# At most four gathers under way in a decoder's routed experts

## What is computed

```python
def _L0_ffn_ref(x, Wg, W1, W2, W3):
    scores = xt @ Wg.T
    topk_scores, topk_idx = jax.lax.top_k(scores, TOP_K)
    gate = jax.nn.silu(jnp.einsum('td,ehd->teh', xt, W1))
    up = jnp.einsum('td,ehd->teh', xt, W2)
    y = jnp.einsum('teh,edh->ted', gate * up, W3)
    onehot = jax.nn.one_hot(topk_idx, E, dtype=x.dtype)
    w = jnp.einsum('tke,tk->te', onehot, topk_scores)
    out = jnp.einsum('te,ted->td', w, y)
    return out.reshape(B, S, D)
...
    x = x + _L0_ffn_ref(_layernorm(x, axis=-1), L0_ffn_Wg, L0_ffn_W1, L0_ffn_W2, L0_ffn_W3)
```

## Time and profile before

| | us |
|---|---|
| median of 3 runs | 1053.18 |
| lowest and highest run | 1051.42, 1053.36 |
| the profiled execution | 1051.36 |
| its span, first to last instruction | 1049.6 |

### The profile page before, as it was taken

The page is one execution under the profiler, slowest core; times in us unless marked ns, Lnnn a source line. Parts: engine busy times, 40 slices in busy tenths (PEclk is TensorE's granted clock), DMA queues, the critical chain, the costliest instruction groups (busy, mean ns, idle before and its releaser), DMA issues. The chain is left out here.

```text
span 1049.6 us, 16519 instructions
## 1 busy us (share of the span) xinstructions
PE 901.8 (86%) x5273; PEld 728.0 (69%) x5274; DVE 640.3 (61%) x1142; ACT 466.1 (44%) x824; POOL 640.3 (61%) x528
## 2 busy tenths in 40 slices
PE   6967667999979999889998899985299999998664
PEld 4534344666856587665787668875299999998654
DVE  4199688887887967976888231573144444443226
ACT  2565755667765568745675123221032333332111
POOL 2178897899977999868998110047465346545250
PEclk8989886999979999979999999988599999999777
DMA  9560022000180000520004000527331333112132
GB/s 319 181 222 0 1 81 81 9 9 1 43 280 1 17 1 1 216 108 17 1 1 161 2 15 2 188 87 228 75 103 53 125 125 125 40 40 75 55 95 96
DMA packets 49405, 86.00 MB, mean 82 GB/s; under 512 B 6420, under 2 KB 39080, under 8 KB 47304
## 3 DMA queue, kind: packets, MB, share of 16 engines
q1 hardware_dynamic: 43352, 66.03, 18.5%
q0 software_dynamic: 6000, 19.29, 6.1%
HBM read 66.16 MB, written 14.55 MB: 77 GB/s over the span
## 5 line engine op out<-in xcount | busy, mean ns | idle before, releaser
L459 POOL TENSOR_TENSOR u<-dtx,b_all 128x512 f32<-128x512 f32 x256 | 332.5, 1310 | 69.0 <-DVE h L722 65.4
L722 DVE TENSOR_TENSOR_SCAN h<-da,u 128x512 f32<-128x512 f32 x256 | 308.8, 1216 | 46.4 <-ACT da L543 21.4
L543 ACT ACTIVATE da<-dt_,a_neg 128x512 f32<-128x512 f32 x256 | 175.0, 690 | 111.1 <-DVE h L722 110.3
L863 PEld LDWEIGHTS ysum<-ident,h 128*128 128x128 f32 x800 | 100.7, 151 | 54.1 <-issue 26.7
L863 PE MATMUL ysum<-ident,h 128*128 128x128 f32 x800 | 117.3, 291 | 17.8 <-DVE h L722 7.7
L1355 ACT ACTIVATE act_<-ps_g 128x352 f32<-128x352 f32 x78 | 36.0, 464 | 150.7 <-PE ps_u L1630 88.9
L1041 PE MATMUL pv<-pT,ctx_n 128*128 128x128 f32 (+1 forms) x832 | 101.3, 275 | 1.1 <-ACT pT L617 1.1
L1041 PEld LDWEIGHTS pv<-pT,ctx_n 128*128 128x128 f32 (+1 forms) x832 | 97.7, 192 | 5.0 <-issue 1.5
L1012 PE MATMUL pa<-ctx_t,xnT_a 128*128 128x401 f32 (+1 forms) x256 | 95.6, 510 | 1.7 <-ACT xnT_a L601 1.4
L1653 PE MATMUL ps_y<-w_hi,hidT_hi 128*128 x234 | 67.1, 287 | 20.6 <-issue 17.8
L1501 DVE TENSOR_TENSOR hid<-act_,ps_u 128x352 f32<-128x352 f32 x78 | 40.3, 517 | 70.5 <-ACT act_ L1355 41.5
(11 more groups left out here) (224 smaller groups left out, 1856.1 us busy)
## 6 DMA issues: line engine op xcount, KB each, us to landing
b_all<-b_dram SPq DMA_DIRECT2D x16, 1024.0 KB, 4.7
ctx_t<-in_ctxT SPq DMA_DIRECT2D x4, 1601.0 KB
ctx_n<-in_ctx SPq DMA_DIRECT2D x4, 1536.0 KB
ffn_sorted<-yg SPq DMA_DIRECT2D x1, 4992.0 KB, 22.6
ffn_sorted<-y_sb SPq DMA_DIRECT2D x39, 128.0 KB
tok_in<-tok SPq DMA_DIRECT2D x35, 128.0 KB, 2.0
mask<-in_mask SPq DMA_DIRECT2D x16, 200.1 KB, 2.4
w_raw<-in_w1T SPq DMA_DIRECT2D x4, 704.0 KB
```

What stands on the lines that cost most here:

```text
L459: nc.gpsimd.tensor_tensor(u[:, i % 2, :], dtx[:, j % 2, :], b_all[:, n, :], ALU.mult).then_inc(u_ok, 1)
L543: nc.scalar.activation(da[i % DS][:], dt_[:, j % 2, :], ACT.Exp, scale=a_neg[:, j, n:n + 1]).then_inc(da_ok, 1)
L722: nc.vector.tensor_tensor_scan(h[:, i % HS, :], da[i % DS][:], u[:, i % 2, :], 0.0, ALU.mult, ALU.add).then_inc(scan_ok, 1)
L863: last = nc.tensor.matmul(ysum[:, t * P:(t + 1) * P], h[:, i % HS, t * P:(t + 1) * P], ident[:], is_transpose=True, start=first and t == 0 ...
```

## The change

```diff
--- before.py
+++ after.py
@@ -1184,6 +1184,7 @@
         PAIRS = 4
         tok_ld = [sem(f"tok_ld{n}") for n in range(PAIRS)]
         AHEAD = 4
+        UNDER_WAY = 4
...
-        low_ld, up_ld, comb = sem("low_ld"), [sem(f"up_ld{g}") for g in range(G // 2)], sem("comb")
+        low_ld, up_ld, comb = [sem(f"low_ld{n}") for n in range(2)], [sem(f"up_ld{g}") for g in range(G // 2)], sem("comb")
...
@@ -1308,8 +1309,8 @@
                 pool.wait_ge(id_ok, 1)
                 for i in range(NT):
 
-                    if i % 2 == 0 and i >= 2 * PAIRS:
-                        pool.wait_ge(tok_ld[i // 2 % PAIRS], gathered(i - 2 * PAIRS))
+                    if i % 2 == 0 and i >= UNDER_WAY:
+                        pool.wait_ge(tok_ld[(i - UNDER_WAY) // 2 % PAIRS], gathered(i - UNDER_WAY))
                     pool.indirect_dma_start(tok[:, i, :], None, xn3_dram,
...
-                def fetch(y, k, done):
+                def fetch(y, k, done, done_before):
                     for g in range(G):
+                        if g % 2 == 0 and g >= UNDER_WAY:
+                            done_before(g - UNDER_WAY)
                         pool.indirect_dma_start(y[:, g, :], None, ffn_sorted,
...
-                fetch(y_one, 0, lambda g: low_ld)
+                fetch(y_one, 0, lambda g: low_ld[g // 2 % 2], lambda g: pool.wait_ge(low_ld[g // 2 % 2], 32 * (g // 4 + 1)))
                 stored(1)
-                fetch(y_two, 1, lambda g: up_ld[g // 2])
+                fetch(y_two, 1, lambda g: up_ld[g // 2], lambda g: pool.wait_ge(up_ld[g // 2], 32))
...
-                    dve.wait_ge(low_ld, 16 * G)
+                    for n in range(2):
+                        dve.wait_ge(low_ld[n], 16 * G // 2)
```

## The result

The changed kernel took 1045.51 us (median of 20 executions; 1037.0 to 1051.89 apart from two, of 1522.42 and 2237.25 us, that the comparison leaves out), the kernel before 1052.7 us beside it (20 executions, 1047.34 to 1054.35). The ratio is 0.9934, 95% interval 0.9916 to 0.9952: 0.7% faster. My forecast of 1054.2 us was wrong, and so was its range, which began at 1048.5.

A forecast was written before the change was run, and what follows sets the result against it. TensorE bounds the expert phase, with three holes under unbroken gathers (56.2 us). Later hole end +4.6, pauses giving back 1.6 and 2.0: +1.0 us, forecast 1054.2 us; own range 1052 to 1055.5, range to hold 1048.5 to 1059.

The forecast's parts named there:

- Three holes bound the kernel: Expert phase: TensorE paces it, except 26.62, 13.96 and 15.58 us when it nearly stands under token, lower and upper gathers.
- itself has the time: GpSimd after the token gathers: a later last gather costs it nothing, since its next work waits until 765.33 for TensorE.
- Lower and upper waits: Twelve new waits in the lower and upper gathers: all already met, cost 0, holes of 13.96 and 15.58 us stay.
- Token waits of 4.6 us: Token gathers beside two weight loads: gathers 6, 12 and 14 wait 2.3, 0.8 and 1.5 us; last starts at 754.4.
- The later end of the hole: Token gathers: Silu again follows the last gather by 3.8 us, so the first hole ends 4.6 us later, +4.6 us.
- What the pauses give back: Token gathers: waits let the other engines catch up, 1.6 us in the first pause and 2.0 us in the later ones.
- 3.0 us of release: Time ScalarE needs to be let go after the last lower gather; taken as what a pause must last to clear everything.
- run-in: Stretch from the first gather after a pause to TensorE's last regular matmul: 12.3, 9.4 and 9.0 us; begins anew at 724.3.
- a standstill clears it: Token gathers: GpSimd's standstill of 5.4 us, from the gather at 711.62 to 717.02, cleared the other engines' delay.
- Rival 1: Token gathers: pauses shorter than the release clear next to nothing, the hole ends later; +2.1 to +5 us, chance 0.34.
- Rival 2: Token gathers: the new run-in lets one more tile through before the stand; 1049.5 to 1051 us, chance 0.14.
- Rival 3: All gathers: missing spacing holds the engines, new waits loosen it everywhere, all holes shrink; halved, about 1025 us, chance 0.12.

The follow-up runs named there:

- half gathers: Kernel before with 64-row lower gathers and tiny operations behind the eighth upper gather: 1053.52 us on a chip with holes, 995.31 and 993.93 us without.
- two under way: Changed kernel with at most two gathers under way, not four: 1051.66 us, ratio 1.0011 with holes; 1050.48 us, 1.0665 without.
- spread kernel: Changed kernel, two token gathers under way, placed between weight splits; lower and upper in groups of four: 993.85 us, 0.9461 with holes; 989.92 us, 1.0042 without.
- plain loads: Kernel before with lower gathers as plain loads without indices and tiny operations between upper gathers: 991.55 and 999.52 us, both on chips without holes.

## Why the prediction was wrong, by its own steps

- **Three holes bound the kernel, and nothing else is late.** Right for the chips with holes. What I said of GpSimd, that it "itself has the time", rests on them: it waits 14.59 us for TensorE only because TensorE stood for 26. In the kernel before on a chip without holes it goes on at once, 0.01 us after the last token gather, and there the waits count in full.
- **Lower and upper waits cost nothing, and their holes stay.** Right: gaps of 0.30 us throughout, holes of 14.6 and 12.8 + 4.3 us, and 1.0001 for these waits alone.
- **Token waits of 4.6 us.** Mis-sized: 10.3, or 9.1 without the usual gaps. Gather 6 waited 4.53 for 2.3, gather 10 3.25 for none, gather 12 1.25 for 0.8, gather 14 1.27 for 1.5. I took the 192nd packet of the queue for the last one of the first four gathers. A pair is complete only when all of its packets are, and those of later gathers can be through before; that is argued from the late releases, no run singled it out. The Trainium skill, "DMA: Bandwidth & Descriptors", section "Queues, rings and completion order", has each of the 16 DMA engines work through a ring of its own and take turns with other queues packet by packet; that fits, since the slowest of the rings then sets a pair's landing, and no view here shows it ring by ring. The last gather came at 757.08, not at 754.4; 7.3 us late and not 9.1, since the first one was 0.6 us early and VectorE's split cost GpSimd 1.2 us less than before.
- **The later end of the hole.** The rule was right, 4.0 us after the last gather for 3.8; with the larger waits it is 7.5 us and not 4.6.
- **What the pauses give back.** The step that failed. I let a pause clear a share of the delay, by its length over the 3.0 us of release, and found 3.6 us, with 6.1 as the end. Two more tiles got through: the fifth tile is 5.2 us early (0.6 of it from the earlier first gather) in spite of an end 7.5 us later, so some 12 us came back, near two tiles (13.5). With pauses of 4.53, 3.25, 1.25 and 1.27 us in a row ScalarE never fell behind: Silu at 728.45 waits for TensorE alone. The run-in then begins anew as I had it, 726.78 to TensorE's hole at 735.34, 8.6 us for 9.0; but I counted one such run-in, where four pauses kept the engines going throughout. How much one pause of 1.3 us clears by itself no run singled out. Nor was "a standstill clears it", read from one gather, safe: in the half gathers' last trace 5.4 us of it cleared nothing. Rival 1, with the same rule of shares at zero, fell with it. Rival 2, a whole tile, had the mechanism and was still too small; it had a chance of 0.14.
- **Rival 3**, spacing helps everywhere: not by the met waits. Yet real spacing does clear all three holes, as the kernel with two under way shows; my argument against it was right only for this change.
- **The new wait.** I named nothing that would be late once the hole is shorter. It was the copy of a tile beside GpSimd's reload of weights, 8.14 us in the chain, and it took back 3.9 of the 5.2 us in the profiled execution. Why other executions keep more, down to 1037 us, stays open: they weren't traced. The last down projection at the lower clock is 1.7 us of it here. A part may come from ahead of the experts, where the first token gather starts anywhere from 686.8 to 696.5 us in the traces of the kernels that are the same up to there, on both kinds of chip.

## What to carry to other kernels

Before a stall of tens of microseconds is charged to the kernel's own order, time the same kernel on another chip: this change is worth -0.7% of the time on one and +1.1% on another. A pause in a stream of gathers can be cheap or dear; what decides is what the issuing engine has to do next and who waits for that. Put the pauses where that engine has slack, here behind the splits of weights that are needed first, and the gain of 5.4% on the one kind of chip costs 0.4 to 0.6% on the other. The spread kernel is right only for these lists of tokens: were the experts ahead of a split to need more tiles than have been gathered, the split would wait for TensorE and TensorE for a gather behind the split, for ever.

## What the hardware showed that I had not expected

- Of the last six sets, two on two chips gave 1052 and 1055.5 us for the kernel before, and four on three chips 986 to 987 us; the chip that came twice was without holes both times, and no chip with holes is on record twice. So that it is the chip, and not what else ran on it or how it was set up at the time, is the nearest reading and not shown. The first two comparisons, both with holes, had 1052.7 and 1051.0. The two traces of the kernel before differ by 68.5 us of span. By the copies of results, the stretch of the token gathers lost 30.4 us over six tiles on the one chip and 2.8 us over twelve on the other; around the lower and the upper hole two tiles each take 16.7 and 16.5 us more than twice 6.74; 5.4 us are an earlier first gather (689.52 for 694.91). Together that is 66.2 of the 68.5 us. The last item isn't the chip's: the spread version had its first gather at 689.44 on the chip with holes. TensorE's granted clock isn't the cause: from 800 to 957 us it is 1.00, the higher of its two levels, in both traces, and its mean of 0.53 from 728 to 756 on the chip with holes goes with TensorE standing there, for 1.00 on the other. Nor is more code loaded: the queues that the profile calls "instruction" move 2 packets from 707 to 756 us with the hole and 3 without; whether such a load, or anything else on its way to these two engines, is held up, no view shows. What differs between the chips stays open.
- On a chip with holes ScalarE is late soon after a row of gathers has begun, and 9 to 12 us into it TensorE nearly stands too, until 3 to 4 us after its last gather, with half the rows in each as with all. They creep rather than stop: ScalarE's Silu at 734.91 above, and TensorE's matmuls in the token hole of the kernel before, which start 1.4 to 3.5 us apart, in steps of 0.70 us:

```profile
738.44 0.37 PE L1653 MATMUL ps_y<-w_hi,hidT_hi 128*128 x1 [1.75 <-issue]
741.24 0.37 PE L1653 MATMUL ps_y<-w_lo,hidT_hi 128*128 x1 [2.43 <-issue]
744.04 0.37 PE L1653 MATMUL ps_y<-w_hi,hidT_lo 128*128 x1 [2.43 <-issue]
```

Four breaks in a row, the last of 1.3 us, kept the engines going, and TensorE stood 8.6 us after the last one; a break of 1.6 us made when they already stood let one Silu through. Whether the reading of indices has a part in it wasn't tried on such a chip: the kernel with plain loads met none.
- Copies of a tile (128 KB) took 6.4 to 8.7 us in the chains of waits where GpSimd's reload of weights ran beside them, on either kind of chip: 8.14 us in the changed kernel, 6.8 to 7.6 in the spread version on the chip with holes, and 7.5 in the kernel before on the third chip. On the first chip the kernel before has none in its chain.
